# A gated cross-attention block on one core: one transfer for the up weights, the gated products on GpSimd, and new orders for all engines

## The reference, cut to what matters

```python
x = x + jnp.tanh(g_xattn[0]) * _L0_xattn_ref(_layernorm(x), fside_BxS2xS2_0, ctx_1024)   # "steps" h and o, 4 batches
x = x + jnp.tanh(g_ffn[0])   * _L0_ffn_ref(_layernorm(x), gate_w, gate_b, val_w, val_b, out_w, out_b)
x = x + jnp.tanh(g_xattn[1]) * _L1_xattn_ref(_layernorm(x), ctx_1024, Wq, bq, Wk, bk)
x = x + jnp.tanh(g_ffn[1])   * _L1_ffn_ref(_layernorm(x), router_w, down_w, up_w)
...
def _expert_forward(xe, guw, dw):          # per batch, 512 tokens
    h = _smooth_quant_linear(xe, guw)      # step h: x 512 wide, weights = fside of the batch
    gate, up = jnp.split(h, 2, axis=-1)
    a = jax.nn.silu(gate) * up             # the product that the change moves
    return _smooth_quant_linear(a, dw)     # step o: weights = ctx of the batch
```

## Time and profile before

| | |
|---|---|
| median of 3 runs (lowest, highest) | 493.36 us (493.35, 498.22) |
| the profiled execution | 493.61 us, its span 491.8 us |
| PE, DVE, ACT, POOL busy | 418.2, 392.4, 354.9, 215.1 us |
| prologue, to the first output matmul | 215.2 us |
| loop and end | 276.6 us |
| bytes moved | 49.77 MB |

### The profile page before, as it was taken

How to read it: one execution, slowest core, us unless ns; L and a number is a source line. 1 busy time by engine, 2 the same in 40 slices (tenths; PEclk the granted TensorE clock), 3 DMA queues, 4 the chain that set the end, 5 groups by cost and what they waited for, 6 DMA issues and landing times.

```text
span 491.8 us, 6980 instructions
## 1 busy us (share of the span) xinstructions
PE 418.2 (85%) x1975; PEld 228.3 (46%) x1975; DVE 392.4 (80%) x985; ACT 354.9 (72%) x587; POOL 215.1 (44%) x317
## 2 busy tenths in 40 slices
PE   0574778995857988788999999999999999999975
PEld 0442645644533734343554455455545554555432
DVE  4777498899887678858788988898889889887642
ACT  1396686799298898977778877787778788777321
POOL 2271553466778555544443334343333333441221
PEclk9875599898999899999999999999999999999999
DMA  8989815386159270232112512221242123113201
GB/s 301 387 245 340 204 43 139 119 207 185 36 177 228 45 139 1 43 64 45 32 34 65 60 37 65 65 53 42 62 72 43 43 65 77 38 49 65 65 7 59
DMA packets 89063, 49.77 MB, mean 101 GB/s; under 512 B 75192, under 2 KB 77496, under 8 KB 88000
## 3 DMA queue, kind: packets, MB, share of 16 engines
q1 hardware_dynamic: 89024, 49.32, 39.7%
HBM read 28.33 MB, written 4.19 MB: 66 GB/s over the span
## 4 chain that ended last, share of the span: by engine, by line
PE 47%; DVE 3%; DMA 2%; ACT 2%; issue 2%; SPq 2%; POOL 0%; POOLq 0%; DVEq 0%; ACTq 0%
PE p_out L1764 10%; PE p_out L1729 9%; PE p_gate L1722 9%; PE p_val L1722 9%; PE p_out L1739 3%; PE p_tr L1704 3%; DMA ws_f<-ws_f 2%; PE p_out L1751 2%; SPq L400 2%; ACT o_q L1216 1%; ACT qT_room L1163 0%; DVE x_all L877 0%; DVE act_f L851 0%; DVE mu L853 0%; ACT p_gate L1323 0%
## 5 line engine op out<-in xcount | busy, mean ns | idle before, releaser
L1722 PE MATMUL p_gate<-gate_t,q_room 128*128 128x512 fp8e4 x256 | 65.7, 379 | 2.5 <-ACT p_gate L1323 2.4
L1722 PE MATMUL p_val<-val_t,q_room 128*128 128x512 fp8e4 x256 | 65.7, 379 | 0.0
L1729 PE MATMUL p_out<-att_t,qT_room 128*128 128x512 f32 x128 | 58.9, 603 | 1.6 <-ACT qT_room L1163 1.6
L1764 PE MATMUL p_out<-out_t,ws_f 128*128 128x512 fp8e4 x256 | 58.4, 379 | 0.4 <-DMA ws_f<-ws_f 0.2
L851 DVE TENSOR_TENSOR act_f<-p_val,ctx_sb 128x512 f32<-128x512 f32 x64 | 44.1, 689 | 8.6 <-PE p_val L1722 5.6
L560 POOL TENSOR_TENSOR rstd<-mv,ln_eps 128x1 f32<-128x1 f32 x48 | 9.4, 196 | 94.6 <-DVE mv L824 94.6
L1323 ACT ACTIVATE p_gate<-w_slots,seed_scale 128x512 f32<-128x512 f32 x64 | 43.5, 682 | 10.2 <-POOL seed_scale L577 8.6
L1308 ACT ACTIVATE ctx_sb<-p_gate,bcol 128x512 f32<-128x512 f32 x64 | 43.6, 682 | 7.0 <-issue 3.4
L853 DVE TENSOR_REDUCE mu<-act_f 128x1 f32<-128x512 f32 x64 | 43.9, 686 | 2.2
L1333 ACT ACTIVATE p_val<-w_in,seed_scale 128x512 f32<-128x512 f32 x64 | 43.3, 680 | 0.1
L1722 PEld LDWEIGHTS p_gate<-gate_t,q_room 128*128 128x128 f16 x256 | 24.8, 98 | 31.7 <-issue 10.5
(11 more groups left out here) (210 smaller groups left out, 959.6 us busy)
## 6 DMA issues: line engine op xcount, KB each, us to landing
att_t<-in_L_ffn_out_w SPq DMA_DIRECT2D x6, 1024.0 KB, 5.0
att_t<-in_L_ffn_gate_w SPq DMA_DIRECT2D x4, 1024.0 KB, 13.0
w_in<-in_fside_BxS2xS SPq DMA_DIRECT2D x4, 1024.0 KB, 7.2
att_t<-in_L_ffn_val_w SPq DMA_DIRECT2D x4, 1024.0 KB, 10.3
out_dram<-x_all SPq DMA_DIRECT2D x16, 256.0 KB, 2.3
x_all<-in_x SPq DMA_DIRECT2D x2, 1024.0 KB, 11.3
x_all<-in_x SPq DMA_DIRECT2D x1, 2048.0 KB, 17.1
ctx_sb<-in_ctx SPq DMA_DIRECT2D x4, 512.0 KB, 4.7
```

The lines of the kernel that those rows point to most:

```text
L1722: last = nc.tensor.matmul(bank[:, c % 2, :], x_t[n % 2][:, k * P:(k + 1) * P], w_t[m][:, k, cols], start=False, stop=k == KD - 1, skip_gro ...
L1729: last = nc.tensor.matmul(p_out[:, 0, :], lt_c[:, k * P:(k + 1) * P], att_t[:, bass.ds((n // T) * (KD * S) + k * S, S)], start=k == 0, sto ...
L1764: last = nc.tensor.matmul(p_out[:, 0, :], p_t[:, k * P:(k + 1) * P], w_t[2][:, k, :], start=k == 0, stop=k == KH - 1)
```

## The change

1. The eight transfers of the up weights (`[128, 4, 16]` each, pieces of 64 bytes) become one of `[128, 8, 64]`, pieces of 256 bytes: a partition now takes rows 4p to 4p + 3 of each expert. An ACT copy (`up_spread`) brings them into the layout for PE's four transposes, and the copy behind the transposes writes with a stride so that `up_t` is as before.
2. `h_hidden`, the 16 products of 128 x 256, moves from DVE's list to POOL's, with its waits.
3. The lists of all five engines are new up to the loop. The loop itself and the end are the same.

```diff
-        up_in = a_f[:, 0:KD * EI].rearrange("p (k e) -> p k e", k=KD)
+        up_in = a_f[:, 0:KD * EI].rearrange("p (e k i) -> p e k i", e=E, k=KD)
+        up_by_k = a_f[:, KD * EI:2 * KD * EI]
...
-        n_small = 2 + 2 + 2 + 2 + E
+        n_small = 2 + 2 + 2 + 3
...
-                    for e in range(E):
-                        sp.dma_start(up_in[:, :, e * I:(e + 1) * I],
-                                     up_w[e].rearrange("(k p) i -> p k i", p=P)).then_inc(small_loaded, 16)
+                    sp.dma_start(a_f[:, 0:KD * EI].rearrange("p (e n) -> p e n", e=E),
+                                 up_w.rearrange("e (p k) i -> p e (k i)", k=KD)).then_inc(small_loaded, 16)
...
                 fside_load(0)
+                w_load(0, 2)
+                w_load(0, 3)
                 w_load(0, 1)
-                w_load(0, 3)
-                w_load(0, 2)
+                small_loads()
+                x_load(1, 1)
                 x_load(2, slice(2, NB))
-                x_load(1, 1)
-                small_loads()
+                val_load(1)
                 val_load(0)
+                fside_load(1)
                 val_load(2)
-                fside_load(1)
-                val_load(1)
                 val_load(3)
...
+                def h_hidden(b, t):
+                    pool.wait_ge(a_silu, T * b + t + 1)
+                    if t == 0:
+                        need(pool, a_q16[1], T * (2 * b - 1))
+                    if b == 0 and t == 0:
+                        pool.wait_ge(prep_tr, 4)
+                    nc.gpsimd.tensor_tensor(a_f[:, t * C:(t + 1) * C], gate_s[:, t % 2, :], h_hs[:, t % 2, C:2 * C],
+                                            ALU.mult).then_inc(a_hidden, 1)
...
-                def h_hidden(b, t):
-                    dve.wait_ge(a_silu, T * b + t + 1)
...
-                    nc.vector.tensor_tensor(a_f[:, t * C:(t + 1) * C], gate_s[:, t % 2, :], h_hs[:, t % 2, C:2 * C],
-                                            ALU.mult).then_inc(a_hidden, 1)
...
                 def small_weights():
+                    act.wait_ge(small_loaded, 16 * n_small)
+                    nc.scalar.activation(up_by_k.rearrange("p (k e i) -> p k e i", k=KD, e=E), up_in, ACT.Copy).then_inc(up_spread, 1)
...
-                    copy(up_t[:, :], p_val[:, 1, :], prep_tr, 4, prep_tr_copied)
+                    copy(up_t[:, :].rearrange("q (p k) -> q k p", k=KD), p_val[:, 1, :].rearrange("q (k p) -> q k p", k=KD), prep_tr, 4, prep_tr_copied)
...
                 w_sum(0, 3)
                 w_sum(0, 1)
+                silu_loaded()
...
                     pe.wait_ge(prep_tr_copied, 2)
+                    pe.wait_ge(up_spread, 1)
                     for k in range(KD):
-                        last = nc.tensor.transpose(p_val[:, 1, k * P:(k + 1) * P], up_in[:, k, :], ident[:, :])
+                        last = nc.tensor.transpose(p_val[:, 1, k * P:(k + 1) * P], up_by_k[:, k * EI:(k + 1) * EI], ident[:, :])
```

More of the change, by code:

```diff
@@ L449, in _ @@
                 integers(1, 2, 1)
+                x_transpose(0)
+                out_b_load()
                 x_transpose(1)
@@ L641, in _ @@
                 o_add(1, 1)
-                q_root(0)
+                h_hidden(2, 2)
+                h_hidden(2, 3)
                 w_round(11)
@@ L648, in _ @@
                 scale_diagonal(1, 2)
+                o_add(1, 2)
+                h_hidden(3, 0)
+                h_hidden(3, 1)
                 q_root(1)
                 q_seeds(0)
-                o_add(1, 2)
+                h_hidden(3, 2)
+                h_hidden(3, 3)
                 o_add(1, 3)
@@ L1417, in _ @@
+                t_context(1)
                 rounded(1, 0, 1)
-                smooth_rows(0, 2)
+                scale_row(1, 0)
+                t_query_key(1)
+                rounded(0, 2, 0)
+                h_silu(1, 2)
+                h_silu(1, 3)
                 t_exponential(1, 0)
                 t_exponential(1, 1)
-                scale_row(1, 0)
+                w_sum(2, 3)
                 t_normalise(1, 0)
-                h_silu(1, 2)
-                h_silu(1, 3)
+                t_normalise(1, 1)
@@ L1801, in _ @@
                 columns(0, 1, 1, 3)
+                columns(0, 1, 0, 0)
+                columns(0, 1, 0, 1)
                 w_total(1)
                 small_weights()
-                w_transpose(4)
-                columns(0, 1, 0, 0)
-                columns(0, 1, 0, 1)
                 columns(0, 1, 0, 2)
                 columns(0, 1, 0, 3)
+                w_transpose(4)
+                products(0, 0, 0)
                 w_transpose(5)
-                products(0, 0, 0)
                 products(0, 0, 1)
+                w_transpose(6)
+                rows(0, 1)
                 products(0, 0, 2)
-                w_transpose(6)
+                w_transpose(7)
                 products(0, 0, 3)
-                rows(0, 1)
-                w_transpose(7)
                 t_context(0)
@@ L1822, in _ @@
                 t_energies(0, 1)
+                columns(0, 2, 1, 0)
                 scale_row(0, 1)
-                columns(0, 2, 1, 0)
                 columns(0, 2, 1, 1)
+                columns(0, 2, 1, 2)
+                columns(0, 2, 1, 3)
+                rows(1, 0)
+                columns(0, 2, 0, 0)
+                columns(0, 2, 0, 1)
                 t_transpose(0, 0)
@@ L1869, in _ @@
                 products(0, 2, 0)
-                columns(0, 3, 0, 1)
                 products(0, 2, 1)
-                columns(0, 3, 0, 2)
-                columns(0, 3, 0, 3)
                 products(0, 2, 2)
                 w_transpose(8)
+                products(0, 2, 3)
+                scale_row(1, 1)
+                rows(0, 3)
                 w_transpose(9)
-                products(0, 2, 3)
-                rows(0, 3)
-                scale_row(1, 1)
                 t_context(2)
+                products(1, 1, 0)
                 t_query_key(2)
-                products(1, 1, 0)
-                products(1, 1, 1)
-                w_transpose(10)
                 t_energies(2, 0)
                 t_energies(2, 1)
+                products(1, 1, 1)
+                scale_row(0, 3)
                 products(1, 1, 2)
-                scale_row(0, 3)
                 products(1, 1, 3)
+                w_transpose(10)
+                t_transpose(2, 0)
                 columns(1, 2, 0, 0)
                 columns(1, 2, 0, 1)
-                t_transpose(2, 0)
                 t_transpose(2, 1)
-                w_transpose(11)
                 t_energies(2, 2)
```

346 lines of the change are left out of this document (165 added, 181 removed).

## The result

The changed kernel took 482.24 us (median of 6 runs, 479.25 to 483.23) against 493.69 us (6 runs, 493.07 to 498.22) of the kernel before: ratio 0.975, 95% interval 0.971 to 0.979. Its profiled execution took 481.64 us with a span of 479.5 us, against 493.61 and 491.8. Some executions of a kernel lie more than 1.5% above its fastest; the ratios here are taken without them, and so is the second median where a kernel has two.

What follows compares the result with a forecast made beforehand. PE bounds the loop (16.71 us a tile), no engine alone the part ahead. Walk 6.7 + products 2.3 + output weights 2.6 = 11.6 us, so 493.6 - 11.6 = 482.0 us; range 475 to 490 us, at 0.8.

Steps and rivals of the forecast that it cites:

- Queue: DMA loads at the start: first two value chunks issued about 27.8 us instead of 31.65, all x in by about 30.
- the walk: Step-by-step reckoning of the start, from the loads to the second batch's last row scale: 6.7 us of lead.
- 3.1 and 4.0 us of these steps: Second batch's PE transposes at 41.2 us instead of 44.30; then value mean, with gamma's group at 48.4 instead of 52.41.
- Maxima, products and rows: Second batch: scale ratio at 55.0 us, 7.7 earlier; scaled activations at 62.3, 7.5 earlier; last row scale at 71.5.
- lead of 6.7 us: Second batch's last row scale on DVE: 71.5 us instead of 78.19.
- The products: Moving 16 products off DVE ahead of the loop: 2.3 us gained, counting only the second batch's four.
- The later eight: Products after the second batch's, 3.5 us of DVE, not counted as gain since ACT is nearer to full there.
- what lies beyond the walk: From the second batch's row scale to the loop: 2.3 us for products and 2.6 for output weights, 4.9 us, called unsure.
- ACT's wait of 5.24 us: ACT waiting until 135.63 us for the output weights' first transpose; half of it, 2.6 us, counted as gain.
- POOL's price: One product on POOL ahead of the loop: 635 ns, together 10.2 us, on an engine with 64 us free there.
- The rival of POOL's line: Ahead of the loop, PE's column transposes wait for products queued on POOL: slower, 497 us; chance 0.08.
- The rule weighed: DVE and POOL operations reading SBUF exclude each other: POOL's products could hold DVE's normalisations about 1 us, giving 483 us.

Runs made afterwards that it cites:

- the products on DVE: Changed kernel with plain copies for its transposing transfers, the 16 products back on DVE, new orders and the up weights' one transfer kept: 486.68 us, ratio 0.984 to the kernel before.
- the orders alone: Changed kernel with plain copies for transposing transfers, products on DVE, up weights in eight transfers without ACT's spread, only the new orders left: 491.01 us, ratio 0.995.
- The kernel before with copies: Kernel before with each of its 128 transposing transfers replaced by a plain copy of the same size: 493.99 us (second median 492.65), ratio 0.999 to the kernel before.
- the changed kernel with copies: Changed kernel, products on POOL, with plain copies in place of its transposing transfers: 481.61 us, ratio 0.975 to the kernel before.

## Why the prediction was right, and where not

- *Queue.* Value chunks at 27.57 us (27.8 was said), no dip at 28 to 32: right. What the walk left out is that the small loads make a dip where they now stand, at 16 to 24 us, with one up transfer too. Fside, the last value chunk and gamma came at 41.61, 46.95 and 49.49 instead of 41.2, 45 and 48.4. PE's transposes were to hang on its scale row; that row ended at 40.44 (39.00 + 1.44), and they waited 1.17 us for fside. Of the 3.1 and 4.0 us of these steps 2.7 and 2.9 came. DVE's wait for x was no loss: it ended at 27.20 us, and at 28.02 in the kernel before.
- *Maxima, products and rows.* Ratio 54.96 (55.0), scaled activations 62.48 (62.3), last row scale 71.33 (71.5). The lead of 6.7 us came as 6.8. But its reasons were mixed up: I put the first lead to the loads and the lists. By the steps of the table 3.4 us of it are the one transfer's and 2.2 the products', and the lists without both give -0.4. Together these are 5.2 and not 6.8, since the last post of the changed kernel stands 1.9 us later in its execution with copies, and that of the kernel before 0.3.
- *The products.* They are worth 5.1 us by the medians (4.4 by the ratios), and the table has 2.2 of it in the walk. Where the rest lies can't be read off: between the runs with the products on DVE and on POOL the last row scales differ by 2.2 us for the second batch's step h, then by 0.5 (first batch, step o), 5.0 (116.56 against 111.59; third, step h), 1.7, 1.0 and 2.3, and the second tile by 2.9. So the 2.3 us for the second batch's four are not confirmed, and in the original pair the lead grows by only 1.0 us from the second to the third batch's row scale of step h (6.8 to 7.8). The later eight are not free either, as I had it: in the stretch of 20.53 against 19.25 us a pair of them kept DVE 1.87 us, and 1.3 us came back when they left.
- *The term that was mis-sized* is what lies beyond the walk, 4.9 us: it came as 13.6 - 6.8 = 6.8. Nor did it come where I had put it: 1.0 us of it is there at the third batch's last row scale of step h, 1.9 at the fourth's, and all 6.8 at the third's of step o. ACT's wait of 5.24 us is gone altogether where I counted half, but that gives nothing by itself: it is gone with the orders alone too, and there the copy behind it starts at 140.02 us and in the base at 135.97. Between the fourth batch's last row scale of step h and the third's of step o the kernel before needs 24.12 us (151.62 to 175.74) and the changed one 19.24 (142.92 to 162.16). The kernel before with copies does the same work there in 21.48 us (151.94 to 173.42), the orders alone in 20.53, with one transfer in 20.53, and with the products on POOL in 19.25. So 1.0 us of the 4.9 are the orders', 1.3 the products', none the transfer's, and 2.6 lie between two executions of the old lists. PE's rows there, of the kernel before

```profile
159.88 1.49 PE L1616 MATMUL p_out<-ident,a_f 128*128 128x128 f32 x8 [1.94 <-DVE o_hs L776]
161.16 3.20 PE L1687 MATMUL p_tr<-rz_diag,e_att 128*128 128x128 f32 x16
```

and with copies

```profile
159.21 1.06 PE L1618 MATMUL p_out<-ident,a_f 128*128 128x128 f32 x8 [1.94 <-DVE o_hs L778]
160.11 1.95 PE L1689 MATMUL p_tr<-rz_diag,e_att 128*128 128x128 f32 x16
```

  The clock granted from 160 to 170 us is 0.83 in the first and 1.00 in the second, and the two rows are 1.7 us longer, which DVE waits for behind them (2.30 us for the energies against 0.67). So of the lead that I read from the profiled executions 1.7 us is the clock of that one execution of the kernel before, which no term of the sum stood for. How little such a pair fixes this term: from the second batch's last row scale to the second tile the original pair needs 153.1 and 146.3 us, and the pair with copies 150.0 and 149.6.
- *POOL's price.* A product takes 729 ns on POOL and not 635, and PE's transposes waited for one only once, 0.7 us. The rival of POOL's line had the mechanism without the condition: DVE waits 3.35 us for a product at 165.81 us, but it would wait as long for its own.
- *The sum.* 13.6 us of lead at the second tile instead of 11.6, 13.8 at 462 us, and 1.5 us of it lost at the end. The sign posts were right up to the row scale; that the time of 482.0 us was met so closely (481.64 profiled) is luck, since these two misses have opposite signs and both have to do with the clock of one execution.
- *The rule weighed.* DVE's normalisations, which the products on POOL should have held up, took 540 ns on average in 24 to 216 us, in the changed kernel as in the run with the products on DVE, and 590 in the kernel before. By the rule of the Trainium skill (SBUF — State Buffer, "Who interferes with whom") they could have cost 1 us; for the normalisations the trace does not show it. Something of that size stands elsewhere: DVE's 16 short scalings (`scale` from `rowmax`, 128x4) took 316 ns on average in the changed kernel, 305 with copies and 241 in the run with the products on DVE, 1.0 to 1.2 us in all. The long ones, 0.26 to 1.19 us instead of 0.17, lie beside POOL's scaling of weights, not beside a product, and the kernel before has them too (341 ns). So it is not shown that the products cause it.

What stays open: both edits in the old lists were not tried, so it is not shown whether the transfer and the products would give their 9.4 us (by the medians) without the new orders, nor which of the many moved lines give the orders' part.

## What to carry to other kernels

Cost a group of small transfers by the stretch in which the queue runs below its pace, and then ask what stands behind it: here a new place changed who paid, and fewer and larger pieces took most of the price away (6.5 us to 2.5). When an operation is moved off an engine that waits now and then, don't count only the stretches where it is fullest: here it paid in others too. A lead read from two profiled executions holds their clocks as well; check its size with medians. When several edits come together, take them away one after the other before giving the gain to any of them.

## What the runs showed of the hardware

*The clock at the end.* At the addition of 462.26 us (476.09 before) the lead is 13.8 us; at the last one, 476.32 against 488.63, it is 12.3. Between them PE's granted clock is 0.70 to 0.73 of 2.4 GHz in the changed kernel, in a mix of its two levels, and 1.00 in the kernel before, with the same instructions and the same wait ahead of them (2.02 us of PE's weight loads, 1.46 of PE, in both). The stretches of the changed kernel, then a row of it:

```profile
464.00:470.00 6.00, 4.25 (x15) 2.95 (x16) 1.35 (x2) 1.41 (x2) 1.00 (x3) 0.70 0.25 91
470.00:476.00 6.00, 5.63 (x18) 1.99 (x15) 2.08 (x10) 0.56 (x2) 1.66 (x1) 0.73 0.00 0
```

```profile
467.87 2.18 PE L1743 MATMUL p_out<-router_down_t,qT_room 128*128 128x136 f32 x8 [0.69 <-ACT qT_room L1164]
```

The same eight matmuls took 1.19 us in the kernel before. No run says why the clock fell in one and not in the other.

*The clock and the spread.* The kernel before gave 490.90 us at a mean granted clock of 0.962 and 497.96 at 0.945 in one series; but 493.40 us came at 0.962 too, so the mean clock is not all of it. In the profiled execution of the changed kernel with copies, 3.4 us above its median, the clock was at half after PE had waited 4.08 us for fside and 1.29 for ACT:

```profile
116.00:120.00 4.00, 3.28 (x15) 3.28 (x16) 3.08 (x12) 3.62 (x7) 1.89 (x3) 0.50 0.25 57
```

```profile
116.72 3.78 PE L1693 MATMUL p_val<-rz_diag,e_att 128*128 128x128 f32 x16 [1.29 <-ACT rz_diag L1255]
```

In the changed kernel as it is the same 16 matmuls took 2.05 us, at the full clock, behind waits of 3.16 and 1.29 us. That this stretch makes up the 3.4 us is not shown: the run with the products on DVE has a clock of 0.50 there too and lies 0.5 us above its median.

*A strided copy.* The copy that writes `up_t` with a stride took 1.12 us, and the plain one in the kernel before 0.60. ACT's other new copy, which spreads the up weights, took 0.61; its target is `up_by_k.rearrange("p (k e i) -> p e k i", ...)`, in the order of `up_in`, and not `p k e i` as the code under "The change" has it.
